# An attention and low-rank-expert block on one core: four stages in turn, rewritten as one interleaved stream

## What is computed

```python
mod = (silu(c) @ wmod).reshape(2, 6, 1, 256)          # sa, ca, ga, sb, cb, gb; |ga|, |gb| >= 0.25
h = layernorm(x) * (1 + ca) + sa
qkv = h @ W_qkv.T + b_qkv                             # 16 heads of 16
attn = softmax(causal(q @ k.T / 4));  o = attn @ v
x = x + ga * (o @ W_out.T + b_out)
h = layernorm(x) * (1 + cb) + sb
h = relu(mole(h, W1, b1, A1, B1, R1))                 # 256 -> 1024
x = x + gb * mole(h, W2, b2, A2, B2, R2)              # 1024 -> 256
# mole: x @ W + b plus three rank-8 adapters, weighted by a softmax over x @ R
```

## Time and profile before

| | us |
|---|---|
| three runs | 1464.73, 1466.1, 1468.05 (median 1466.1) |
| profiled execution, span from first to last instruction | 1465.0 |
| PE busy | 1309.6 (89%) |
| DVE busy | 1022.1 (70%) |
| ACT busy | 773.8 (53%) |
| POOL busy | 172.6 (12%) |

### The profile page before, as it was taken

The page is one execution under the profiler, slowest core; times in us unless marked ns, Lnnn a source line. Parts: engine busy times, 40 slices in busy tenths (PEclk is TensorE's granted clock), DMA queues, the critical chain, the costliest instruction groups (busy, mean ns, idle before and its releaser), DMA issues. The chain is left out here.

```text
span 1465.0 us, 25799 instructions
## 1 busy us (share of the span) xinstructions
PE 1309.6 (89%) x8432; PEld 679.2 (46%) x8432; DVE 1022.1 (70%) x1862; ACT 773.8 (53%) x1009; POOL 172.6 (12%) x101
## 2 busy tenths in 40 slices
PE   4993899999999998999998999999994599999997
PEld 3872223333333333333433433433221588888886
DVE  4893997886886885886887688688300466666664
ACT  2771004665665664666565666566793244444443
POOL 1468100000000000000000000000001122222221
PEclk8996557999999999999999999999997699999999
DMA  6345400002102101200210300200003102222200
GB/s 204 123 165 165 131 1 11 21 16 58 33 18 50 40 17 35 56 19 15 65 26 4 74 18 16 63 6 5 10 8 91 44 1 58 58 57 57 57 14 29
DMA packets 75812, 71.07 MB, mean 49 GB/s; under 512 B 17816, under 2 KB 68704, under 8 KB 75688
## 3 DMA queue, kind: packets, MB, share of 16 engines
q1 hardware_dynamic: 75688, 69.51, 16.9%
HBM read 47.57 MB, written 21.23 MB: 47 GB/s over the span
## 5 line engine op out<-in xcount | busy, mean ns | idle before, releaser
L854 DVE TENSOR_REDUCE mx<-ps 128x1 f32<-128x512 f32 (+3 forms) x1120 | 692.2, 669 | 170.8 <-PE ps L726 105.8
L808 ACT ACTIVATE prob<-ps 128x1024 f32<-128x1024 f32 (+3 forms) x640 | 546.7, 895 | 413.8 <-PE ps L751 260.0
L723 PE MATMUL ps<-kst,qst 96*128 96x512 bf16 (+3 forms) x1280 | 426.4, 374 | 28.4 <-DMA kst<-qk_parts 24.3
L747 PE MATMUL ps<-qst,kst 99*128 99x512 bf16 (+3 forms) x1280 | 362.2, 355 | 11.2 <-issue 7.5
L763 PE MATMUL ps<-prob,vw 128*32 128x512 f32 (+3 forms) x2560 | 303.8, 547 | 0.2
L723 PEld LDWEIGHTS ps<-kst,qst 96*128 96x128 bf16 x1280 | 120.7, 99 | 334.7 <-DVE mx L854 244.9
L747 PEld LDWEIGHTS ps<-qst,kst 99*128 99x128 bf16 x1280 | 118.9, 99 | 147.5 <-ACT prob L808 51.1
L751 PE MATMUL ps<-mask_k,ident_bf 128*128 128x128 bf16 x512 | 106.2, 227 | 0.0
L726 PE MATMUL ps<-mask_q,ident_bf 128*128 128x128 bf16 x512 | 106.0, 232 | 0.0
L926 POOL COPY vw<-v_nat 128x1024 f32 (+1 forms) x8 | 8.3, 1044 | 766.3 <-PE ps L763 766.3
L763 PEld LDWEIGHTS ps<-prob,vw 128*32 128x32 f32 x2560 | 51.0, 109 | 102.0 <-issue 79.6
(11 more groups left out here) (144 smaller groups left out, 1429.5 us busy)
## 6 DMA issues: line engine op xcount, KB each, us to landing
qk_parts<-parts SPq DMA_DIRECT2D x32, 384.0 KB, 2.9
qst<-qk_parts SPq DMA_DIRECT2D x192, 64.0 KB, 2.6
kst<-qk_parts SPq DMA_DIRECT2D x192, 64.0 KB, 2.5
xs<-in_x SPq DMA_DIRECT2D x16, 512.0 KB, 6.3
o_rows<-o_sb SPq DMA_DIRECT2D x128, 32.0 KB, 1.7
o_raw<-o_rows SPq DMA_DIRECT2D x16, 256.0 KB
rd<-rden_rows SPq DMA_DIRECT2D x16, 256.0 KB
out<-y SPq DMA_DIRECT2D x8, 512.0 KB, 3.2
```

Source lines behind the costliest of these rows:

```text
L723: last = pe.matmul(at, q[0:QK_ROWS, J, h0 + h, i % 4 * P:(i % 4 + 1) * P], k[0:QK_ROWS, cb, h0 + h, 0:width], start=True, stop=not diagonal)
L747: last = pe.matmul(ps[:, h, 0:width], kst[c][0:ST_ROWS, t // 4, h, t % 4 * P:(t % 4 + 1) * P], qst[c][0:ST_ROWS, J, h, skip:BLK], start=Tr ...
L808: act.activation(prob[:, n % P_BUFS, 2 * pair:2 * pair + 2, 0:width], ps[:, 2 * pair:2 * pair + 2, 0:width], ACT.Exp).then_inc(exp_done, 1)
L854: dve.tensor_reduce(mx[:, h0:h0 + nh, i % 4, cb], ps[:, bank, 0:nh * width].rearrange("p (h x) -> p h x", h=nh), AX, ALU.max).then_inc(max ...
```

## The change

Nearly all of the program is new. After the setup there is one block and no loop: everything is laid out at build time on a common scale of *steps*, one step being one attention tile of 128 keys by 512 queries for four heads.

- The 32 units (sequence, chunk J of 512 queries, group of four heads) are run in causal order, chunk by chunk, so 320 steps in all. Each step has two logit events (`logits(s, 0)`, `logits(s, 1)`), each of two heads.
- q and k are kept as float32 rows in three slots of 16 (hi, hi, lo against hi, lo, hi), so a head has 48 rows and two rows for the maximum, 50 in place of 99. Two heads stand on top of one another, on partitions 0 to 49 and 64 to 113, and each matmul takes one half of the partitions, into a PSUM bank of its own. The masks become `pick` matmuls of 64 rows, two for each head.
- The maxima of the next unit are spread over the steps of the unit at hand (`pair_steps`). Their PSUM ring is three banks (`M_BANKS`), which also serves the projections; two slots of two banks (`A_SLOTS`) serve the logits, the turns, q and k and the hidden layer. One bank holds the output.
- First and last stage are cut into blocks of 256 tokens (16 each), and each block into pieces (`s_...`, `f_...`), put at fixed steps (`S_START`, `F_START` and the offsets). Four first-stage blocks come before step 0; the last two blocks of the last stage end 45 steps after step 320.
- The inverse root moves to POOL (`pow` and one Newton step), the splitting in high part and remainder moves from ACT and DVE to POOL (`two_parts`), b1 moves into the low-rank matmul, the softmax sum is inverted on DVE as 128x512 elements for each block, and the w1, w2 split is done by POOL at step -8.

The core of the diff:

```diff
-KT = [(J, t) for J in range(NJ) for t in range(4 * (J + 1))]
-P_BUFS, PV_LAG = 4, 2
-S_BUFS = 3
+UNITS = [(b, J, g) for b in range(B) for J in range(NJ) for g in range(NH // GH)]
+STEP = [(u, t) for u, (_, J, _) in enumerate(UNITS) for t in range(4 * (J + 1))]
+TB = 256
+ROWS = 3 * HD
+ST_ROWS = ROWS + 2
+K_BUFS, Q_BUFS, V_BUFS, P_BUFS = 7, 3, 6, 3
+PV_LAG = 2
+MAX_LEAD = 3
+A_SLOTS, M_BANK, M_BANKS, O_BANK = 2, 4, 3, 7
+BEGIN, END = -24, NSTEP + 50
+S_START = [-24, -20, -15, -10, 14, 22, 58, 66, 112, 126, 146, 153, 174, 182, 214, 228]
+F_START = [24, 39, 56, 74, 104, 122, 168, 186, 204, 222, 240, 258, 276, 294, 328, 339]
+S_PIECES = {"s_load": -4, "s_stat": 0, "s_turn": 2, "s_qk0": 5, "s_qk1": 6, "s_v": 7, "s_store": 8}
+F_PIECES = {"f_load": -5, "f_norm": 0, "f_proj": 2, "f_stat": 4, "f_turn": 6, "f_route": 8, "f_exp": 9,
+            "f_gate": 10, "f_zturn": 12, "f_hid0": 13, "f_hid1": 14, "f_hid2": 15, "f_hid3": 16,
+            "f_down0a": 18, "f_down0b": 19, "f_down1a": 20, "f_down1b": 21, "f_exp2": 22, "f_gate2": 23,
+            "f_zturn2": 24, "f_low": 25, "f_out": 26}
+def unit_pairs(u):
+    J = UNITS[u][1]
+    full = [(c, i, slice(p, p + 1), BLK, False) for c in range(J) for i in range(4) for p in range(2)]
+    diagonal = []
+    for r in range(4):
+        together = 2 if r < 2 else 1
+        diagonal += [(J, r, slice(p, p + together), (r + 1) * P, True) for p in range(0, 2, together)]
+    return full + diagonal
...
+            def _(pe):
+                def logits(s, p):
...
+                    if event >= A_SLOTS:
+                        pe.wait_ge(a_free, event - A_SLOTS + 1)
...
+                    for a in range(2):
+                        half = slice(64 * a, 64 * a + ST_ROWS)
+                        last = pe.matmul(ps[:, bank + a, 0:width], kst[half, slot, p, t % 4 * P:(t % 4 + 1) * P],
+                                         qst[half, u % Q_BUFS, p, skip:BLK], start=True, stop=(t < 4 * J))
+                    if t >= 4 * J:
+                        for w, a in ((0, 0), (0, 1), (1, 0), (1, 1)):
+                            half = slice(64 * a, 64 * a + 64)
+                            last = pe.matmul(ps[:, bank + a, 0:P], pick[half, w - a + 1], mask_k[half, w - a + 1],
+                                             start=False, stop=(w == 1))
...
+                def maximum(u, k):
...
+                    for p in range(both.start, both.stop):
+                        at = (p - both.start) * width
+                        for a in range(2):
+                            half = slice(64 * a, 64 * a + ROWS)
+                            last = pe.matmul(ps[:, M_BANK + banks[a], at:at + width],
+                                             qst[half, u % Q_BUFS, p, i * P:(i + 1) * P],
+                                             kst[half, K_SLOT[u, c], p, 0:width], start=True, stop=not diagonal)
...
+                for s in range(BEGIN, END):
+                    first, second = groups(s)
+                    if 0 <= s < NSTEP:
+                        logits(s, 0)
+                    if s in TURN_AT:
+                        turn_maxima(TURN_AT[s])
+                    for u, k in first:
+                        maximum(u, k)
+                    if 0 <= s - PV_LAG < NSTEP:
+                        values(s - PV_LAG)
+                    if 0 <= s < NSTEP:
+                        logits(s, 1)
+                    for u, k in second:
+                        maximum(u, k)
+                    for piece, n in JOBS[s]:
+                        if piece in pieces:
+                            pieces[piece](n)
...
+            def _(act):
...
+                def f_hid(n, j):
+                    event = A_AT[f"f_hid{j}", n]
+                    if 4 * n + j:
+                        act.wait_ge(hid_done, 4 * n + j)
+                    act.wait_ge(a_full, event + 1)
+                    act.activation(hidf[:].rearrange("p m t -> p (m t)"), ps[:, event % A_SLOTS * 2, :],
+                                   ACT.Relu).then_inc(a_free, 1)
...
+            def _(dve):
...
+                def f_norm(n):
+                    dve.wait_ge(fo_in, 16 * 3 * KC * (n + 1))
+                    dve.reciprocal(fd[:], fd[:]).then_inc(rec_done, 1)
...
+            def _(pool):
...
+                def split_weights():
+                    pool.wait_ge(ffn_in, 16 * 3)
+                    for full, (hi, lo) in ((w1_full, w1_p), (w2_full, w2_p)):
+                        link(pool.tensor_copy(hi[:], full))
+                        pool.tensor_tensor(lo[:], full, hi[:].bitcast(F32), ALU.subtract).then_inc(split_done, 1)
...
+                def two_parts(parts, src, ready):
+                    link(pool.tensor_copy(parts[0][:], src))
+                    pool.tensor_tensor(parts[1][:], src, parts[0][:].bitcast(F32), ALU.subtract).then_inc(ready, 1)
```

More of the change, by code:

```diff
@@ L39 @@
 T = B * S
-BLK = 512
-TT = BLK // P
-NBLK = T // BLK
 EPS = 1e-5
 NEG = -3.0e38
+BLK = 512
+NJ = S // BLK
+NCHUNK = B * NJ
 GH = 4
[L46 to L50, removed]
-KT = [(J, t) for J in range(NJ) for t in range(4 * (J + 1))]
-NKT = len(KT)
-P_BUFS, PV_LAG = 4, 2
[L54 to L70, removed]
@@ new lines, with groups, rings, take @@
+PAIRS_AT = pair_steps()
+TURN_AT = {FIRST[u] - MAX_LEAD: u for u in range(NU)}
+STEP_OF_PAIR = {pair: s for s, pairs in PAIRS_AT.items() for pair in pairs}
+def groups(s):
+    pairs = PAIRS_AT[s]
+    half = (len(pairs) + 1) // 2
+    return pairs[:half], pairs[half:]
+def rings():
+    a_at, m_at, used, held, last = {}, {}, [0] * M_BANKS, {}, M_BANKS - 1
+    def take(name):
+        nonlocal last
+        last = next(b for b in ((last + d) % M_BANKS for d in range(1, M_BANKS + 1)) if b not in held.values())
+        m_at[name] = (last, used[last])
+        used[last] += 1
+    for s in range(BEGIN - 5, END):
+        first, second = groups(s)
+        if 0 <= s < NSTEP:
+            a_at["exp", s, 0] = len(a_at)
+        if s in TURN_AT:
+            take(("turn", TURN_AT[s]))
+        for u, k in first + second:
+            take(("max", u, k, 0))
+            take(("max", u, k, 1))
+        if 0 <= s < NSTEP:
+            a_at["exp", s, 1] = len(a_at)
+        for piece, n in JOBS[s]:
+            if piece in A_PIECES:
+                a_at[piece, n] = len(a_at)
+            if piece in M_PIECES:
+                take((piece, n))
+                if piece in M_HELD:
+                    held[M_HELD[piece], n] = last
+            held.pop((piece, n), None)
+    return a_at, m_at
@@ L397, in build_program @@
[L397 to L419 removed]
+        qst = sb(whole, "qst", [P, Q_BUFS, 2, BLK], F32R)
@@ new lines, in product, with a_bank @@
+                def product(out, lhs, rhs, chunks, stop=True):
+                    for k in range(chunks):
+                        for n, (i, j) in enumerate(PASSES):
+                            last = pe.matmul(out, lhs(i, k), rhs(j, k), start=(k == 0 and n == 0),
+                                             stop=(stop and k == chunks - 1 and n == len(PASSES) - 1))
+                    return last
+                def a_bank(piece, n):
+                    event = A_AT[piece, n]
+                    if event >= A_SLOTS:
+                        pe.wait_ge(a_free, event - A_SLOTS + 1)
+                    return event % A_SLOTS * 2
```

1678 lines of the change are left out of this document (715 added, 963 removed).

## The result

The changed kernel takes **1732.7 us** (median) beside 1467.1 for the kernel before, measured together: a ratio of 1.180, 95% interval 1.178 to 1.183. It is 18% slower; 1255 was forecast, and the range ended at 1420. Its four runs took 1730.6, 1731.5, 1733.9 and 1769.6 us; the last ran at a lower clock, and the ratio leaves it out. The profiled execution took 1730.6 us, with a span of 1728.9.

What follows compares the result with a forecast made beforehand. Attention was taken to be bound by PE's matmul columns. Head 96, PE in the steps 939, DVE's pieces 100, steps where J rises 40 and tail 85 sum to 1260, stated as 1255 us; own range 1180 to 1350, 8-in-10 range 1140 to 1420.

Steps and rivals of the forecast that it cites:

- The single prices: Costs per instruction: reciprocal 3.2 us on DVE, values 1.00 on PE, ACT 690 in all.
- the big term: Logits and maxima on PE, two heads at a time on separate row halves: 1280 pairs at 0.23, 294 us.
- The first rival: Pairs of logits and maxima on PE: the halves do not overlap, 1485 us, 1% slower; chance 0.09.
- What the sum of one engine leaves out: PE and DVE tied by a three-bank ring: steps cost the larger of the two, about 2.2 us without a piece.
- DVE's pieces and the steps where J rises: Additions to the 320 steps: 100 us for DVE's pieces, some 40 for longer maxima falling into a shorter unit.
- the price of a change of tiling: PE, at pieces: 0.06 us a change, some 300 pieces give 36 us; bounds nothing and 72.
- the 0.23 of a pair: Two float32r matmuls of 512 columns on separate row halves of PE cost 0.23 us together; 0.46 without overlap.
- head and tail: Before and after the 320 steps: head 96 us, tail 85 us.
- the third rival: POOL's links come late, stopping ACT and PE in six steps of each block: +96, 1350 us; chance 0.14.
- the clock: PE's granted clock was expected over 0.9 in the 320 steps, with nothing added for a lower level.
- the 939 of the sum: PE's work inside the 320 steps: 294 + 61 + 272 + 276 + 36 = 939 us.
- The second rival: PE's clock falls in stretches that DVE sets, some 30% of the steps: 1360 us; chance 0.12.

Runs made afterwards that it cites:

- number 7: All 16 last-stage blocks moved behind step 320, against the changed kernel: 1960.5 us in one run, the steps 1157.8 us.
- number 1: Logits and maxima operands read as bfloat16 in place of float32r, against the changed kernel: 1604.1 us, 128.6 less.
- number 4: DVE's reductions of the maxima read 64 of up to 512 columns, q scaled by 1/64, against the changed kernel: 1566.6 us, 166 less.
- number 2: The price list: 7 rows of 24 matmuls or groups added behind the changed kernel's last step, for each price alone: 1764.1 us in one run.

## Why the prediction was wrong

**What held.** The single prices: the reciprocal 3.34 us (3.2 forecast), the values 0.98 from the first to what follows (1.00), ACT 685 us (690), and two halves of the rows side by side at the price of one, which was the big term. The first rival, that the halves do not overlap, is wrong although its time, 1485, was the nearest of all. The Trainium skill, "TensorE: Matmul & The Clock Gate", Part 3, has tiles in separate row groups run concurrently. The price list agrees, with 0.233 us for a pair and 0.227 for one.

**Step that failed, 1: "What the sum of one engine leaves out".** It said that a step without a piece is "about 2.2 us on both", as steps cost the larger of the two engines. The three above last 3.02 us, 72 such steps that ran wholly at the full clock 2.84 in the mean (logits to logits, in the timeline), and 2.7 had been named as the bound beyond which the forecast is wrong. Four reductions are 2.63 us where the average of 3.75 at 0.60 had made 2.25: the 0.60 came from 21 in a row without a break, and two by two they take 1.3 a pair. The ring adds 0.39 in which DVE has nothing: with two banks to a pair, three banks are one and a half pairs, and PE, in order, stands with them. The loop that this makes was worked out from the timeline; the same step falls to 2.81 with shorter pairs and to 2.56 with shorter reductions, as a loop through both engines would. Shortening the reductions was worth 166 us; of DVE's pieces and the steps where J rises the forecast had 140 in its sum, as additions to a step that was itself too short. The bare steps are less than half of the overrun: 120 steps without a piece on PE average 3.70 us at either clock, 180 us too much in all (the 4.15 in number 7 is near to what the 57 without a piece on any engine take), and the 199 with one 5.26, where the sum leaves them 4.1, which is 231.

**Step that failed, 2: the price of a change of tiling**, "0.06 a change, and some 300 pieces give 36 us", and with it the 0.23 of a pair. There and back costs 0.33 us at the values, where the 1.00 held 0.14, and 0.41 at the pieces, where 0.12 was counted. A step with a piece has two runs of pairs, so both are paid: 320 x 0.19 and some 200 x 0.29 make about 120 us more. A third place was not seen: some 330 pairs stand behind masks, and there a float32r pair of maxima is followed after 0.31 us, a bfloat16 one after 0.23 (medians in the timelines of the changed kernel and of number 1), which is some 27 us. The bfloat16 pairs took 80 us of this out of PE's work (busy time by clock 1141 x 0.88 = 1004 for 1084); the rest of their 129 us came with the higher clock. The Trainium skill, "TensorEngine Tiling (Array Packing)", section "Tiling Modes", says that a change of mode drains the engine; the trace agrees in so far as each change costs time. The price that I worked out from the old values was too small by a factor of three. One reason stands in the trace of before, 600 to 604 us:

```profile
600.59 0.38 PE L723 MATMUL ps<-kst,qst 96*128 96x512 bf16 x1
600.90 1.07 PE L763 MATMUL ps<-prob,vw 128*32 128x512 f32 x8
```

The matmul ahead of the values takes 0.31 us in place of 0.22: the way into the values is paid there, and I had looked for it in their 1.00 alone.

**Step that failed, 3: head and tail**, 125 and 112 us for 96 and 85. Waits of PE from 0 to 125 and from 1617 to 1729 us:

```profile
PE ps L635 <- POOL sx L1023: 40.2, 4, 12.9
```
```profile
PE ps L616 <- POOL oT_lo L1031: 20.7, 2, 18.6
```

By these both are chains through POOL; no run took POOL's work away to test it. Standardising 256 columns takes POOL 1.25 us, which no row had shown, and POOL was busy 562 us for 440. Inside the steps POOL hardly stops PE (under 10 us), so the third rival was right in its engine and wrong in its place.

**Step that failed, 4: the clock**, which stood in the sum at nothing. By the estimate of number 4 PE's work in the steps is 1306 x 0.83 = 1084 us at the full clock, 145 over the 939 of the sum. The other 222 us the lower level added. PE was idle for 187 us where the sum had 140. These three, 145, 222 and 47, make up the 414. The second rival had 30% of the steps at the lower level; it was a third, though its 1360 us were far off. The lower level follows PE's waiting: with lighter DVE work the clock rose by itself, to 0.89 and 0.93. What it costs by itself stays open: raised by filling, it gave 31 us in one run and at most 25 in another, but the filling took PE's time as well.

**What stays open.** With three costs out, 1443 us are still 188 over the forecast: 50 of them in head and tail (231 for 181), 137 in the steps. There PE is idle for 140 us, as the sum had it. It is busy for 1076 us against 939, at a clock of 0.93; by the estimate above 61 us of the difference are PE's own work, for changes of tiling without their loads, and 76 the lower level. A fourth bank for the maxima would have tested the ring directly; all eight are in use, and it was not tried.

## What to carry to other kernels

A packed matmul is cheap in a row of its like and dear as a visitor: count the changes of tiling on the path and price them there and back, from the matmul ahead of the change as well as from the one behind it. Where two engines pass work through a ring in pairs, a step is not the larger of their sums: look how many whole hand-overs the ring holds, and what the in-order engine has queued behind the one that waits. And interleaved stages cost more than their work on the bound engine: here 335 us for 224, in one run and by the forecast's prices.

## What the hardware showed that was not expected

- Float32r of 512 columns, one after another at the full clock, takes 0.23 us on 128 rows, on 64 rows of one half, and for both halves together (number 2); there and back between column quarters and row halves 0.33 us with float32r, 0.22 with bfloat16, and 0.41 between whole rows and row halves.
- A DVE cast of 16 elements took 1.27 us where it began with a POOL product of 1.26 (1277.62 above), and 0.17 elsewhere; over the 32 of them some 10 us. Ten of the casts began while POOL was at an instruction with two inputs of 512 or more columns, and each ended 0.03 us after it. Where one began first, it was not held up:

```profile
907.47 0.17 DVE L869 CAST mparts<-negm 128x16 fp32r<-128x16 f32 x1
907.49 1.28 POOL L1061 TENSOR_TENSOR fo<-fo,fd 128x512 f32<-128x512 f32 x1 [18.93 <-DVE fd L908]
```

  The Trainium skill, "SBUF — State Buffer", section "SBUF: two separate sides", has an exclusive lock on a port pair that the two engines share, for some forms of DVE instruction, held by the one that starts first; the rows agree, though no run here took POOL's work away to show it.
- The lower clock lasted for tens of microseconds in which PE had work nearly throughout. Window of the changed kernel, where J rises:

```profile
1306.00:1354.00 48.00, 42.74 (x200) 17.58 (x198) 28.82 (x62) 17.52 (x21) 8.60 (x12) 0.50 0.13 36
```

PE is busy for 42.7 of 48 us, in pairs, values and pieces with single waits of 0.4 to 1.6 us for DVE between them, and is granted 0.50 all the time. The Trainium skill, "TensorE: Matmul & The Clock Gate", section "A second HAM failure mode", tells of a clock that goes up and down where PE idles often between groups of matmuls; the granted clock in the slices of the profile's page agrees with that, and this window adds that it can also stay down.
